# An adaLN transformer block on one core: the first norm of each half and five units of the first softmax are transposed by transfers instead of on TensorE

## The reference, cut to what matters

```python
# x (2, 1024, 256); attention matrices (2, 1024, 1024); hidden layer 1024
sa, ca, ga, sb, cb, gb = (silu(c) @ wmod).reshape(2, 6, 1, 256) ...   # six rows per batch
ga, gb = sign * maximum(abs, 0.25)
h = layernorm(x) * (1 + ca) + sa
Q, K, V = split(h @ c_attn_w + c_attn_b)
base_A  = softmax(Q[:, :, :128] @ K[:, :, :128].T * SCALE)      # first softmax
cam_ctx = base_A @ V[:, :, :128]
bias    = tanh(cam_ctx * cam_gate) @ K[:, :, :128].T * SCALE * layer_weight
A       = softmax(Q @ K.T * SCALE + bias)                       # second softmax
x = x + ga * ((A @ V) @ c_proj_w + c_proj_b)
h = layernorm(x) * (1 + cb) + sb
x = x + gb * (gelu(h @ proj1.T + b1) @ proj2.T + b2)
```

## Time and profile before

| | us |
|---|---|
| median of three runs | 309.2 |
| the profiled execution: its own time | 309.08 |
| its span in the profile | 307.3 |
| PE busy | 300.9 |
| DVE busy | 223.4 |
| ACT busy | 158.7 |
| POOL busy | 107.4 |

### The profile page before, as it was taken

The page is one execution under the profiler, slowest core; times in us unless marked ns, Lnnn a source line. Parts: engine busy times, 40 slices in busy tenths (PEclk is TensorE's granted clock), DMA queues, the critical chain, the costliest instruction groups (busy, mean ns, idle before and its releaser), DMA issues.

```text
span 307.3 us, 5121 instructions
## 1 busy us (share of the span) xinstructions
PE 300.9 (98%) x1920; PEld 273.1 (89%) x1920; DVE 223.4 (73%) x439; ACT 158.7 (52%) x268; POOL 107.4 (35%) x131
## 2 busy tenths in 40 slices
PE   7999999999999999999999999999999999999995
PEld 5889989898998988998899888898998999899895
DVE  5776789886899889768733789787789994951631
ACT  2676666553344548708912486645253445941920
POOL 4526734244457548035011132130011344414211
PEclk9999999999999999999999999999999999999999
DMA  7920200736655000010011000004656400001001
GB/s 223 376 87 1 56 15 0 265 79 217 196 192 149 3 0 2 0 53 17 1 36 34 3 0 0 2 0 103 208 170 218 125 2 1 1 2 67 4 17 52
DMA packets 16665, 22.89 MB, mean 74 GB/s; under 512 B 1664, under 2 KB 13696, under 8 KB 16640
## 3 DMA queue, kind: packets, MB, share of 16 engines
q1 hardware_dynamic: 16640, 22.56, 23.1%
HBM read 13.64 MB, written 8.39 MB: 72 GB/s over the span
## 4 chain that ended last, share of the span: by engine, by line
PE 86%; DVE 5%; DMA 2%; ACT 2%; issue 2%; SPq 1%; POOL 1%; DVEq 0%; POOLq 0%
PE a_ps L196 13%; PE a_ps L198 13%; PE a_ps L197 13%; PE s_ps L196 12%; PE s_ps L198 12%; PE s_ps L197 12%; PE t_ps L1230 5%; PE t_ps L1157 2%; DMA wp_raw<-wp 2%; DVE nmax L852 2%; DVE pt_lo L846 1%; ACT prob L603 1%; ACT pt_hi L588 1%; PE a_ps L1139 1%; PE s_ps L1088 1%
## 5 line engine op out<-in xcount | busy, mean ns | idle before, releaser
L603 ACT ACTIVATE prob<-s_ps,nmax 128x1024 f32<-128x1024 f32 x32 | 35.8, 1118 | 48.5 <-DVE nmax L852 48.4
L852 DVE TENSOR_REDUCE nmax<-s_ps 128x1 f32<-128x1024 f32 x32 | 39.0, 1217 | 12.0 <-PE s_ps L198 11.9
L588 ACT ACTIVATE pt_hi<-t_ps 128x512 fp32r<-128x512 f32 x64 | 34.9, 596 | 24.7 <-PE t_ps L1230 20.2
L846 DVE TENSOR_TENSOR pt_lo<-t_ps,pt_hi 128x512 fp32r<-128x512 f32 x64 | 41.1, 683 | 3.8 <-ACT pt_hi L588 3.7
L196 PE MATMUL s_ps<-k_hi,q_hi 128*128 128x512 f32 x96 | 38.2, 398 | 0.0
L198 PE MATMUL s_ps<-k_hi,q_lo 128*128 128x512 f32 x96 | 37.6, 392 | 0.0
L197 PE MATMUL s_ps<-k_lo,q_hi 128*128 128x512 f32 x96 | 37.5, 391 | 0.0
L196 PE MATMUL a_ps<-v_hi,pt_hi 128*128 128x256 f32 x128 | 36.4, 284 | 0.0
L196 PE MATMUL a_ps<-w_hi,pt_hi 128*128 128x256 f32 x128 | 36.4, 284 | 0.0
L197 PE MATMUL a_ps<-w_lo,pt_hi 128*128 128x256 f32 x128 | 36.2, 283 | 0.0
L198 PE MATMUL a_ps<-w_hi,pt_lo 128*128 128x256 f32 x128 | 36.2, 283 | 0.0
(11 more groups left out here) (158 smaller groups left out, 760.6 us busy)
## 6 DMA issues: line engine op xcount, KB each, us to landing
turned<-prob SPq DMA_DIRECT2D x48, 128.0 KB, 2.9
f32s<-turned SPq DMA_DIRECT2D x12, 512.0 KB, 3.6
w_raw<-w_t SPq DMA_DIRECT2D x2, 1024.0 KB, 6.2
out<-x_all SPq DMA_DIRECT2D x16, 128.0 KB, 1.7
x_all<-x SPq DMA_DIRECT2D x4, 256.0 KB, 4.8
wmod_raw<-wmod SPq DMA_DIRECT2D x1, 1024.0 KB, 8.3
x_all<-x SPq DMA_DIRECT2D x2, 512.0 KB, 10.1
wmod_raw<-wmod SPq DMA_DIRECT2D x1, 512.0 KB, 5.1
```

The lines of the kernel that those rows point to most:

```text
L588: A(pt_hi[:, (u // 2) % 2, 4 * g:4 * g + 4, (u % 2) * P:(u % 2 + 1) * P], t_bank(b, "p", 2 * u + g)[:, :].rearrange("p (t n) -> p t n", n= ...
L603: A(dst, src, ACT.Exp, bias=nmax[:, u:u + 1], accum_out=rsum[:, u:u + 1]).then_inc(exp_ready, 1)
L846: V.tensor_tensor(pt_lo[dst], t_bank(b, "p", 2 * u + g)[:, :].rearrange("p (t n) -> p t n", n=P), f(pt_hi[dst]), ALU.subtract).then_inc(pt ...
L852: V.tensor_reduce(nmax[:, u:u + 1], s_ps[u % 2][:, :], AX.X, ALU.max, negate=True).then_inc(nmax_ready, 1)
```

## The change

- `DMA_CAM`: in batch 0 the first-softmax units 4 and 6, in batch 1 the units 2, 4 and 6, go by transfers. They land in `xn` (a third landing buffer), after `divide_by_sum`, and are turned by DVE, split and used one slot later than before (`s - 3` in place of `s - 2`). `turn_order` swaps them with the unit behind them in `T_JOBS`.
- `DMA_NORMS`: the norms (0, 3), (1, 0), (1, 1), (1, 3) go by transfers, landing in the halves of `f32s`. Their `h_transpose` calls are gone; DVE turns them (`turn_norm`), and the next `norm_apply` waits until the norm has left `xn`. The norm's last turn now stands behind `ffn_gated` calls in DVE's list.
- SP's queue becomes: transfers of the batch's units, norm 3, norm 0 of the next batch, four result tiles, norm 1, the other result tiles.
- The four late query and key projections of each batch are split by POOL (`qk_split_pool`), not by DVE.
- The FFN weights are loaded from ACT's queue in slot 6, not from SP's.
- Prelude: the constants' columns come first, then the first four token tiles in one transfer, the first modulation weights in two, the query and key weights behind the projection weights; the modulation runs in another order over four PSUM banks; half of one weight split moves from POOL to DVE; the bias row (four matmuls) moves from slot 2 to the prelude.

```diff
+DMA_NORMS = ((0, 3), (1, 0), (1, 1), (1, 3))
+DMA_CAM = ((4, 6), (2, 4, 6))
+TRIPS = ([("p", 0, u) for u in (*DMA_CAM[0], *DMA_UNITS)] + [("h", 0, 3), ("h", 1, 0), ("h", 1, 1)]
+         + [("p", 1, u) for u in (*DMA_CAM[1], *DMA_UNITS)] + [("h", 1, 3)])
...
+        def landing(d):
+            return xn[:, :, :].rearrange("p t e -> p (t e)") if d == 2 else quad[:, d, :]
...
-            load_x(0, 0, 2)
             sp.dma_start(cols_sb[:, :], cols).then_inc(cols_in, 16)
-            load_x(1, 2, 2)
-            sp.dma_start(wmod1_raw[:, :, :], wm[:, :, 0:2 * E]).then_inc(wmod1_in, 16)
-            sp.dma_start(wattn_raw[:, :, 0:2 * E], wa[:, :, 0:2 * E]).then_inc(wqk_in, 16)
+            load_x(0, 0, TH)
+            for k in range(EC):
+                sp.dma_start(wmod1_raw[:, k, :], wm[:, k, 0:2 * E]).then_inc(wmod1_in[k], 16)
             sp.dma_start(wvt_raw[:, :, :], wv_t.rearrange("(c p) n -> p c n", p=P)).then_inc(wvt_in, 16)
             sp.dma_start(wp_raw[:, :, :], wp.rearrange("(c p) n -> p c n", p=P)).then_inc(wp_in, 16)
+            sp.dma_start(wattn_raw[:, :, 0:2 * E], wa[:, :, 0:2 * E]).then_inc(wqk_in, 16)
...
+            def send_probs(b, u):
+                k = TRIPS.index(("p", b, u))
+                wait(sp, pnorm_ready if u < T else exp_ready, b, u + 1)
+                write_rows(k, prob[:, u % 3, :])
+                if by_dma(b, u - 2) and u not in (T, T + 1):
+                    wait(sp, t_psum, b, turned_by(b, u - 2))
+                elif u >= T:
+                    wait(sp, qklo_pool, b, 4)
+                elif b == 0:
+                    wait(sp, ht_psum, 0, 4)
+                read_rows(k)
...
             for b in range(B):
-                for u in DMA_UNITS:
-                    write_probs(b, u)
-                    read_probs(b, u)
+                for u in (*DMA_CAM[b], *DMA_UNITS):
+                    send_probs(b, u)
+                send_norm(b, 3)
+                if b + 1 < B:
+                    send_norm(b + 1, 0)
                 for t in range(T):
+                    if t == TH and b + 1 < B:
+                        send_norm(b + 1, 1)
...
+            def qk_split_pool(b, j):
+                m, h = QK_JOBS[j]
+                hi, lo = (q_hi, q_lo) if m < 2 else (k_hi, k_lo)
+                dst = (slice(None), m % 2, slice(h * HALF, (h + 1) * HALF))
+                wait(pool, qk32_ready, b, j + 1)
+                G.tensor_scalar(hi[dst], f32s[:, j % 3, :], 1.0, 1.0, ALU.mult, ALU.mult).then_inc(qkhi_pool, 1)
+                wait(pool, qkhi_pool, b, j - 3)
+                G.tensor_tensor(lo[dst], f32s[:, j % 3, :], f(hi[dst]), ALU.subtract).then_inc(qklo_pool, 1)
...
+                    if b == 0 and s == 6:
+                        load_ffn()
+                    if s - 3 < T and by_dma(b, s - 3):
+                        prob_high(b, s - 3)
...
+            def turn(trip, kind, jobs, signal):
+                d, count = back(*trip)
+                dve.wait_ge(probs_back[d], count)
+                for g in range(2):
+                    if (w := read_out(T_JOBS, T_READ_OUT, (trip[1], kind, jobs[g]))) is not None:
+                        dve.wait_ge(*w)
+                    V.transpose(t_bank(trip[1], kind, jobs[g])[:, :].rearrange("p (a i c) -> p i a c", a=TH, i=Q),
...
# vector, slots: the transposed first-softmax units, at the end of slot u + 3
+                    if s - 3 < T and by_dma(b, s - 3):
+                        turn_probs(b, s - 3)
+                        prob_low(b, s - 3)
...
# vector, FFN
-                    if n == 3:
+                    if n == 2:
                         norm_apply(b, 3)
+                    if n == HC - 2 and b + 1 < B:
+                        norm_apply(b + 1, 0)
+                ffn_gated(b, 0)
+                ffn_gated(b, 1)
+                turn_norm(b, 3)
+                h_split(b, 6)
+                h_split(b, 7)
+                ffn_gated(b, 2)
+                ffn_gated(b, 3)
                 if b + 1 < B:
                     norm_stats(b + 1, 1)
...
                 for n in range(HC, 2 * HC):
+                    if n == HC and b + 1 < B:
+                        turn_norm(b + 1, 0)
                     gelu_low(b, n)
...
                 if b + 1 < B:
+                    qk_split(b + 1, 0)
+                    ffn_gated(b, TH)
+                    ffn_gated(b, TH + 1)
+                    turn_norm(b + 1, 1)
                     h_split(b + 1, 2)
                     h_split(b + 1, 3)
...
# tensor
-                    if s >= 2 and s - 2 not in DMA_UNITS:
+                    if s >= 2 and not by_dma(b, s - 2):
                         transpose_probs(b, s - 2)
...
                 ffn_down(b, 1, 0, 4)
-                h_transpose(b, 6)
-                h_transpose(b, 7)
                 ffn_down(b, 0, 4, HC)
...
-                if b + 1 < B:
-                    h_transpose(b + 1, 0)
-                    h_transpose(b + 1, 1)
                 for n in range(HC, 2 * HC):
                     ffn_up(b, n)
                 if b + 1 < B:
-                    h_transpose(b + 1, 2)
-                    h_transpose(b + 1, 3)
                     qk_project(b + 1, 0)
```

More of the change, by code:

```diff
@@ L221, in adaln_block_kernel @@
         for b in range(B):
-            A_JOBS += [(b, "v", t) for t in range(3 if b else TH)]
-            A_JOBS += [(b, "gate", 0)] if b == 0 else []
+            A_JOBS += [(b, "v", t) for t in ((0, 1, 2) if b else (0, 2, 3))]
+            A_JOBS += [] if b else [(0, "row", 0), (0, "gate", 0)]
             for s in range(UNITS):
@@ L228, in adaln_block_kernel, with turn_order, turned_by @@
                       "wvp": wv_lo_ready, "gate": gate_copied, "row": row_added}
+        def turn_order(b):
+            order = list(range(UNITS))
+            for u in DMA_CAM[b]:
+                order[u], order[u + 1] = u + 1, u
+            return order
+        def turned_by(b, u, g=1):
+            return 2 * turn_order(b).index(u) + g + 1
         T_JOBS = []
@@ L256, in read_out, with v_bank, mod2_psum_columns, sent @@
             s = signals[kind]
-            return s, b * per.get(s, 0) + k + 1
+            return s, b * per.get(s, 0) + (turned_by(b, k // 2, k % 2) if kind == "p" else k + 1)
+        def v_bank(b, t):
+            return s_bank(2) if (b, t) == (0, 1) else a_bank(b, "v", t)
         MOD_N = 64
[L261 to L271, removed]
+        MOD1_BANKS = (a_ps[1][:, :], s_bank(3), s_bank(0), s_bank(1))
+        def mod2_psum_columns():
+            return t_bank(0, "mod", 1)[:, 0:4 * MOD_N].rearrange("p (v a b) -> p a b v", b=B, v=4)[:, 0, :, :]
+        def sent(*trip):
+            return 16 * Q * (TRIPS.index(trip) + 1)
+        def back(*trip):
+            d, _, n = slot(trip)
+            return d, 16 * n
+        def slot(trip):
+            def home(t):
+                return 2 if t[0] == "p" and t[2] < T else t[2] % 2
+            d = home(trip)
+            same = [t for t in TRIPS[:TRIPS.index(trip) + 1] if home(t) == d]
+            return d, same[-2] if len(same) > 1 else None, len(same)
+        def by_dma(b, u):
+            return ("p", b, u) in TRIPS
+        def landing(d):
+            return xn[:, :, :].rearrange("p t e -> p (t e)") if d == 2 else quad[:, d, :]
         def gelu_of(n):
@@ L663, in _ @@
                         softmax_exp(b, s)
-                    if s >= 2:
+                    if s >= 2 and not (s - 2 < T and by_dma(b, s - 2)):
                         prob_high(b, s - 2)
@@ L1042, in modulation_second @@
                 t_free(0, "mod", 1)
-                modulation(1, range(4)).then_inc(mod2_psum, 1)
+                for v in range(4):
+                    for k in range(EC):
+                        last = modulate(t_bank(0, "mod", 1)[:, v * MOD_N:(v + 1) * MOD_N], wmod2_raw, E + v * P, k)
+                last.then_inc(mod2_psum, 1)
             def gate_rows():
```

257 lines of the change are left out of this document (136 added, 121 removed).

## The result

The changed kernel takes **306.6 us** (median of 19 runs, 305.3 to 309.0) where the kernel before takes 309.0 (19 runs, 308.5 to 312.2): a ratio of 0.992, interval 0.990 to 0.994. The prediction was 301.7 with 299.8 to 306.3. Of the 7.4 us forecast, 2.3 came; it is a miss on the high side. The gain is clear of the noise, but it is less than the 1% (3.1 us) that the prediction asked for before it would say "faster". Two of the 19 runs (308.3 and 309.0) had a granted clock of 0.994, the others 0.999 or more. The profiled execution took 306.63, span 304.8.

A forecast was written before the change was run, and what follows sets the result against it. The prediction took PE to bound the kernel, nearly always busy, with DVE close behind. It summed 309.1 - 7.8 (transposes) - 0.5 (prelude) + 0.6 (slots) + 0.3 (FFN) = 301.7 us, range 299.8 to 306.3.

The forecast's parts named there:

- prelude, with bias row and loads: Before the first scores: reordered loads let the first projection start earlier, -0.5 us; bias row move and ACT's loads cost nothing.
- four norms: Norm transposes leave PE at 0.87 us each; one +0.3 stall where the next batch's norm_apply delays gelu_low(7).
- POOL's splits: Late projection splits on POOL: 0 in the sum, DVE delays of 1.3 us a batch only in the range.
- five units: First-softmax units' transposes leave PE at 0.87 us each, less stalls of 0.3 us in each batch's attention.
- the norm trips and their 0.9 us in hand: FFN, norm 3: transferred data ready at about 136.4 us, PE wants it at 137.3, so covered by 0.9 us.
- the trips of the first softmax: First-softmax units' HBM trips take 8.0 us, covered by about 14.7 us of slots, 5 us or more to spare.
- The slots: Attention around slot 10: PE may wait for unit 8's prob_low; +0.3 us per batch, sum 0.6, bounds 0 to 2.7.
- lower case: In the attention slots DVE keeps up with the earlier PE because slots 5 and 6 lost their splits; loss 0.
- upper case: DVE gets no earlier and two added turns use up its wait: stalls of 0.9 us in batch 0, 1.8 in batch 1.
- The first rival: DVE becomes the bound in the first softmax, with POOL's delays added: 304 to 306 us, chance 0.20.
- the DVE case: The rival with DVE as first-softmax bound, 304 to 306 us, chance 0.20; its top, given as 306.3, ends the range.
- The slower rival: Late trips stop DVE's in-order list, holding up the next row maximum, exponential and scores: about 315 to 324 us, chance 0.06.

The follow-up runs named there:

- e7: Changed kernel with no units and no norms by transfers, late projections split by DVE again, so only prelude, bias row and FFN loads remain: 307.9 us, ratio 0.998.
- e8: e7 with the four norms by transfer added; no units by transfer, late splits on DVE: 305.1 us, ratio 0.988.
- e2: Changed kernel with all norms transposed on PE again, units and POOL's splits kept: 310.0 us, ratio 1.003.
- e1: Changed kernel without the five first-softmax units by transfer; norms, POOL's splits and prelude kept: 303.8 us, ratio 0.983.
- e4: Changed kernel with q_update ahead of row_recip in DVE's list, in the slots that lost a prob_low: 302.7 us, ratio 0.979.
- e3: Changed kernel with the late query and key splits back on DVE instead of POOL: 308.0 us, ratio 0.996.
- e5: e4 with ACT making prob_high(2) ahead of cam_tanh in slot 5 of batch 1: 302.4 us, ratio 0.980.
- e9: e5 with units by transfer in batch 1 alone; units 4 and 6 of batch 0 back on PE: 302.8 us, ratio 0.978.
- e11: e5 with POOL making the power for norm 2's rstd ahead of its two additions in the last slot: 301.8 us, ratio 0.975.
- e12: e11 with unit 15's row maximum ahead of unit 13's turn on DVE in the last slot: 301.25 us, ratio 0.974.
- e10: e5 with the reads of the second softmax's trips (units 8 to 13) issued by GpSimd, not SP: 305.3 us, ratio 0.987.

## Why the prediction was wrong

The change taken in order, with each part's term; medians, and in brackets the stretch where it says another thing:

| part | predicted | measured | from |
|---|---|---|---|
| prelude, with bias row and loads | -0.5 | -0.8 | e7 |
| four norms | -3.5 + 0.3 | -2.9 | e8 to e7 (3.3 from e2) |
| POOL's splits | 0 | -1.3 (-0.8) | e1 to e8 |
| five units | -4.35 + 0.6 | **+2.85** (+1.9) | after to e1 |

**Right.** The count of removed matmuls (72), the turns at 0.70, the prelude, the norm trips and their 0.9 us in hand, the trips of the first softmax (no DVE wait for one of their landings in the changed kernel), and that POOL's later splits would hold up no division. Its sign "PE busy about 293" did not come: 295.5.

**The step that failed** is "The slots", +0.3 for each batch. It looked for the stall at one place, unit 8's `pt_lo` in slot 10, and in one currency, DVE's busy time. Its lower case, near which it put the term, reads: "DVE follows, because the splits of slots 5 and 6, which kept its row maxima late, are gone, and nothing is lost". Even its upper case, 2.7 for both batches, is short of what the term came to: 4.35 + 2.85 = 7.2 us (6.3 by the stretch). What the runs show instead:

1. *Order.* Moving `prob_low` out of slots 6 and 8 (and 4 in batch 1) uncovers `row_recip`'s wait for the exponential, 1.27 us, ahead of `q_update`. The prediction named what DVE got and lost, never what stood behind the removed instruction in the list.
2. *The block.* The prediction had it, from the earlier trace rows: up to 0.7 to 1.3 us on each update, twice a batch. It kept it out of the sum because the maxima, the turns and `prob_low` work on PSUM and stay steady. They did; what it left out is that PE waits for the update itself, and for what stands behind it. (Two such delays a batch make up to 2.6 us, where its range has 1.3.) In slot 6 the update takes 3.85 us for the 1.71 that it takes unblocked (e4), because the division, released by the same reciprocal, starts beside it, and the split follows. The kernel before had the block there too, on one instruction (L826 took 1.24, the update 2.54), and no split of POOL followed it; without the split the changed kernel has 2.53 (e3). The Trainium skill, page SBUF — State Buffer, section Who interferes with whom, calls the shared pair an exclusive lock for the whole instruction and says that issue order decides who blocks. The rows agree: two of the four instructions lost 0.80 and 1.05 us, L918 ends with the division, L922 with the split, the division itself took 1.27 for its mean of 1.14 where L916 was ahead of it, and e4 frees them by order alone.
3. *The consumer.* PE's scores of units 8 and 10 need the update; the prediction listed only `pt_lo` and `prob` as places to look at. The wait on `q_lo`, 1.8 us in the view and 2.5 by the starts, was not on its list of signs.

e4 changes just points 1 and 2 and brings 4.0 of the 6.6 us between forecast and result for the units (by the stretch 3.3 of 5.7).

**The rest, some 2.5 us,** is lost mostly in the second softmax. From unit 8's attend to ffn_up 0 e5 takes 1.5 us longer than e1 in batch 0 and 0.9 in batch 1; ahead of it nearly all of the gain is kept (1.6 of 1.74 us and 2.6 of 2.61). In that stretch of batch 0 DVE is busy for 33.4 of 38.7 us, and its turns wait for landings, 3.8 us in both batches. Ahead of it PE gained 1.7 by the two units of batch 0, and 0.3 or less reached the end (e9). The first rival ("DVE becomes the bound") had the right engine and nearly the right time (304 to 306), but put the bound in the first softmax by a sum of work, and there DVE's work fell. By these waits the bound stands one stage later, and includes SP's ordered trips; that is argued and not shown by a kernel of its own. e11 and e12 recover together 1.2 us there by order (1.0 by the stretch), the second part within the uncertainty. What SP's order costs by itself stays open: e10 meant to show it and disturbed POOL. That POOL's splits would be worth 1.3 us was not foreseen: the forecast took DVE's relief as hidden behind a full PE. By the marked starts the 0.8 us of the stretch all lie in batch 1, between unit 8's attend and ffn_up 0 (36.31 us in e1, 37.11 in e8), and so behind the slots that the splits had left; which wait gives them was not followed further.

The sum's other terms hold. Two small slips: PE's longest wait before was the 1.2 us at its very first matmul (L1061), not 1.1, and the prediction's own upper terms add up to 306.4 for the DVE case.

The slower rival (315 to 324, late trips) did not happen in the change. Its mechanism, DVE's list stopped at a landing with the next maximum behind it, is the one that e12 works against, with a price of 1.12 us and not of 2 to 6.

## What to carry to other kernels

When an instruction leaves an in-order list, look at what stood behind it: if the next one waits for another engine, the removed work was that wait's cover, and the wait becomes a cost at once; put independent work in its place. Where DVE and GpSimd work in turn on SBUF data, ask which semaphore starts the GpSimd instruction: one released by a reciprocal that stands just before a chain of DVE instructions meets that chain each time, and moving the release behind the chain removes it without taking work away. A stage gain is worth something only up to the next stage's bound, so follow it to the end of the pipeline before adding it up.

## What the runs showed of the hardware

- DVE instructions of 0.42, 0.29 and 0.42 us took 1.22, 0.59 and 1.47 beside GpSimd instructions (1.27, 0.78, 1.29), each ending about when GpSimd's did; the same pair in e4 apart in time took the short values.
- GpSimd's split of 128x512 kept its 0.62 + 1.29 us in most places, but its cast took 0.78 at 55.45 (changed kernel) and 0.87 at 85.03 (e10) next to DVE: the block goes both ways.
- A trip of 512 KB through HBM took 4.8 us from the first write's issue to the read's (1.9 of it four issues) and 3.3 from there to landing, in the middle of the second softmax (e5); one trip there took 5.9 to the read, where the prediction had 4.4. From one read to the next it was 5.1 to 5.3, once 6.3, because in SP's one list the read waits for the writes and the next writes stand behind it.
- A read issued by GpSimd held it 0.53 to 0.79 us (e10), one issued by SP held SP 0.34; median landing 3.8 (e10) and 3.7 us (e5).
- In e3, batch 1, TensorE ran no matmul for 2.35 us, and right after it the granted clock stood at 0.50 (1.2 GHz) for 3.4 us; a matmul of 512 columns then stepped by 0.43 us for 0.23.
